# First layer's attention: scores by quarters of the array, one score bank per head

## The chip, the cores and the metric

The kernel is one program on one core of a Trainium2 chip. Its time is the device time of an execution in microseconds; of several runs the median counts. A profile of one execution gives each instruction its start and length.

## What is computed

The reference is a network of two layers on `x` of 4 x 1024 tokens with 128 features. Each layer has an attention and a mixture of experts, each behind a LayerNorm whose output is scaled and shifted per batch entry and each gated before it is added back. The change touches the first layer's attention alone: 16 heads of 64 features, a window of 64 tokens back, and a bias that grows with the distance.

```python
q = rmsnorm(x @ wq.T, q_norm_w)          # over all 16 * 64 features
k = rmsnorm(x @ wk.T, k_norm_w)
v = x @ wv.T
scores = einsum('bhqd,bhkd->bhqk', q, k) * HD ** -0.5
scores = scores + slopes[:, None, None] * dist      # dist = key - query
scores = where((dist > 0) | (dist < -64), -inf, scores)
out = einsum('bhqk,bhkd->bhqd', softmax(scores), v) @ wo.T
```

## The kernel before, in words

The whole program keeps `x` in SBUF and runs stage after stage; between two stages all engines meet. The stage here is `window_attention_stage`. It treats two heads at a time, a *pair*: 64 features of head 0 on partitions 0 to 63, 64 of head 1 on partitions 64 to 127. There are 4 batch entries x 8 pairs = 32 pairs. A pair's 1024 queries fall into 16 blocks of 64, and a block sees the 128 keys that end with its own 64 (`kk`, `k_pad`, has 64 columns of zeros ahead of the first key). Four blocks are one *step*; a pair has four steps (r = 0 to 3 in the code, steps 1 to 4 in the text), the stage 128.

Each engine's program is written out as a loop over g, the number of the step, and works at several steps at once:

- TensorE (PE), in iteration g: the scores of g (L734); the projections for the next pair (`project`, L714 and L717: two of q in step 1, two of k in step 2, half of v in steps 3 and 4 each); the transposes of the probabilities of g - 2 (L745, `probsT_ps`); the output products of g - 3 (L760, `o_ps`, each head in its half of the array's columns, on its 64 partitions of the result); after step 4 of a pair the wo products of the pair before (L773).
- ScalarE (ACT): the evacuation of the projections from PSUM (q L819, k L824, v L826), then the four exponentials of g (L869, with their sums), then the copy `oT` of the output products of g - 3 (L877).
- VectorE (DVE): the second head's half of the q evacuation (L892), then bias, mask and row minimum of the scores of g (they are held negated) in one custom instruction per block with a read-out of the minimum behind it (L960, `s_biased` and `s_min`), the reciprocal of the sums of g - 1 (L966), the copy of the transposed probabilities of g - 2 (L972).
- GpSimd (POOL): the normalisation of the probabilities (L989). SyncE: a DMA that shifts v by 64 tokens (`v_shift`).

The order of work is thus fixed by the loops; semaphores (`s_mm`, `biased`, `exped`, `rsum`, `normed`, `turned`, `pt_out`, `pv_mm`, `o_out`, `a_out`) hold an engine until another has counted far enough. Into the pairs of batch entries 1 to 3 the loops also sow the next stage's work on the batch entry before (`routed`, `route`: LayerNorm statistics, POOL's rstd at L145, the normalised tiles `hk` at L155, transposes at L680, the router's logits and tables), at fixed steps.

The scores of a block are one 128 x 128 product. Its weights are a block-diagonal table `qbd` (`q_bd`): columns 0 to 63 hold head 0's queries in partitions 0 to 63, columns 64 to 127 head 1's queries in partitions 64 to 127, the other two quarters are zero. So a product yields 64 queries of head 0 on partitions 0 to 63 and 64 of head 1 on 64 to 127, against 128 keys. ACT writes one quarter and DVE the other; POOL has zeroed the table ahead of the stage. The four products of a step fill one PSUM bank of two (`sp_[g % 2]`):

```python
if g >= 2:
    pe.wait_ge(biased, g - 1)
for i in range(4):
    j = 4 * r + i
    m = nc.tensor.matmul(sp_[g % 2][:, i, :], qbd[:, h % 2, j, :],
                         kk[:, h % 2, BLK * j:BLK * j + P], start=True, stop=True)
```

In the trace a float32 product has two records of PE (and two weight loads, PEld).

Of the kernel before, what the change touches and what calls it, by code (L numbers as in the profile page):

```python
# [35 lines left out]
NBLK = T // BLK  # L36
RMS_EPS = 1e-6
# [530 lines left out]
def window_attention_stage(nc, K, A, gram, hq, hk, M, N1, N2, aff_in):  # L568
# [3 lines left out]
    with ExitStack() as st:  # L572
# [4 lines left out]
        nbias = K.sb("nbias", [P, PAIRS, P], ctx=st)  # L577
# [3 lines left out]
        qbd = K.sb("q_bd", [P, 2, NBLK, P], ctx=st)  # L581
# [14 lines left out]
        def fill(pool):  # L596

            for n, dst in enumerate((qbd[:].rearrange("p a b c -> p (a b c)"), kk[:, :, 0:BLK], vs[0:BLK, :, 0, :])):
# [12 lines left out]
        def scale_q(dve):  # L611
# [21 lines left out]
        (h_in, p_mm, a_out, q_out, v_sh0, v_sh1, s_mm, biased, exped, rsum, normed, turned, pt_out, pv_mm, o_out,  # L633
         wo_mm, wo_gated, x_added, prob_set, scaled, shifted) = K.sems(
            st, "win", "h_in", "proj_mm", "act_out", "q_out", "v_shift_even", "v_shift_odd", "score_mm", "biased",
            "exp", "rsum", "normed", "turned", "probsT_out", "pv_mm", "o_out", "wo_mm", "wo_gated", "x_added", "probs_set",
            "scaled", "shifted")
# [31 lines left out]
        with nc.Block() as block:  # L669
            @block.tensor  # L670
            def _(pe):
# [24 lines left out]
                def project(n):  # L696
# [3 lines left out]
                    if n >= 2:  # L700

                        hh, uu = units[n - 2]
                        pe.wait_ge(a_out, n - 1)
                        if uu in (0, 1):
                            pe.wait_ge(q_out, 2 * hh + uu + 1)
# [18 lines left out]
                for g in range(G + 4):  # L724
                    h, r = divmod(g, GRP)
                    if g < G:
                        if r == 0:
                            pe.wait_ge(a_out, out_count(h, 3))
                            pe.wait_ge(q_out, 2 * h + 2)
                        if g >= 2:  # L730
                            pe.wait_ge(biased, g - 1)
                        for i in range(4):
                            j = 4 * r + i
                            m = nc.tensor.matmul(sp_[g % 2][:, i, :], qbd[:, h % 2, j, :],  # L734
                                                 kk[:, h % 2, BLK * j:BLK * j + P], start=True, stop=True)
                        m.then_inc(s_mm, 1)
# [10 lines left out]
                    if 3 <= g < G + 3:  # L747
# [31 lines left out]
            def _(act):  # L779
# [26 lines left out]
                def evacuate(n):  # L806
# [49 lines left out]
                for g in range(G + 3):  # L856
# [4 lines left out]
                    if g < G:  # L861
                        act.wait_ge(biased, g + 1)
                        if g == 0:
                            act.wait_ge(prob_set, 1)
                        if g >= 3:
                            act.wait_ge(turned, g - 2)
                        for i in range(4):
                            own = slice(BLK if g % GRP == 0 and i == 0 else 0, P)
                            r = nc.scalar.activation(pr[:, g % 3, i, own], sb_[:, g % 2, i, own], ACT.Exp, scale=-1.0,  # L869
# [12 lines left out]
            def _(dve):  # L882
                v = nc.vector

                def evacuate(n):
                    h, u = units[n]
                    if u not in (0, 1):
                        return
                    dve.wait_ge(p_mm, n + 1)
                    if u == 0 and h >= 2:  # L890
                        dve.wait_ge(s_mm, GRP * (h - 1))
# [4 lines left out]
                for n in range(6):  # L896
                    evacuate(n)
                v.memset(pr[:, :, 0, 0:BLK], 0.0).then_inc(prob_set, 1)
# [49 lines left out]
                for g in range(G + 2):  # L948
# [3 lines left out]
                    for n in unit_steps(g):  # L952
                        evacuate(n)
                    if g < G:
                        dve.wait_ge(s_mm, g + 1)
                        if g >= 2:
                            dve.wait_ge(exped, g - 1)
                        for i in range(4):
                            own = slice(BLK if 4 * r + i == 0 else 0, P)
                            q = v.tensor_tensor_reduce(sb_[:, g % 2, i, own], sp_[g % 2][:, i, own],  # L960
                                                       nbias[:, h % PAIRS, own], 1.0, 3e38, ALU.add, ALU.min,
                                                       mn[:, g % 4, i:i + 1])
# [15 lines left out]
            def _(pool):  # L978
                M.constants(pool)
                for g in range(G):  # L980
# [9 lines left out]
                    if g % 2 == 1 and g // 2 < FILLS:  # L990
                        if g == 1:
                            pool.wait_ge(filled, 4)
# [1505 lines left out]
def constants():  # L2498
# [5 lines left out]
    neg = np.empty((2, BLK, PAIRS, P), np.float32)  # L2504
    ok = (dist <= 0) & (dist >= -WIN)
    for h in range(H0):
        neg[h % 2, :, h // 2, :] = np.where(ok, -slopes[h] * dist, 1e30)
# [8 lines left out]
    return {"identity": np.eye(P, dtype=np.float32), "neg_bias": neg.reshape(P, PAIRS, P),  # L2516
# [46 lines left out]
```

## Time and profile before

| | us |
|---|---|
| runs shown: median of 3 (lowest, highest) | 2058.07 (2057.89, 2059.19) |
| span of the profiled execution, first to last instruction | 2056.4 |
| PE / PEld busy | 1579.5 / 917.7 |
| DVE / ACT / POOL busy | 1339.0 / 1135.7 / 550.2 |
| first and last score product of the stage start at | 87.1 and 606.6 |

The profiled execution's own device time is not listed apart from the three runs; its span lies 1.5 to 2.8 us below them. A share of busy time is a mean over the whole span. What an engine is worth in one stage is read in that stage, from the work in order of time: a row there has the start and length of an instruction (or of several alike, "x8"), its engine and line, what it writes and reads, and in brackets how long its engine sat idle before it and which instruction ended that.

### The profile page before, as it was taken

The page shows a single profiled execution, that of the slowest core. Times are in us where ns is not written, and L with a number is a line of the kernel's source. Part 1 is how long each engine was busy: PE and PEld are TensorE (multiplying, and loading weights), DVE is VectorE, ACT ScalarE, POOL GpSimd, SP SyncE. Part 2 cuts the span into 40 slices and gives each one's busy share as a digit, 9 for nine tenths or more (in the row PEclk, how much of TensorE's full clock was granted, in tenths as well). Part 3 has the DMA queues.
Part 4 walks back from the last instruction along what each step waited for, and adds up shares of the span by engine and source line. Part 5 has one row for each costly group of instructions (what it writes and reads, how often), then busy time and mean ns, then how long its engine had stood idle before and what let it go on. Part 6 is the DMA issues. An engine that isn't in the chain of part 4 may idle for free. (4 is left out here: it accounts for less than half of the span.)

```text
span 2056.4 us, 34421 instructions
## 1 busy us (share of the span) xinstructions
PE 1579.5 (77%) x11512; PEld 917.7 (45%) x11512; DVE 1339.0 (65%) x3318; ACT 1135.7 (55%) x2965; POOL 550.2 (27%) x615
## 2 busy tenths in 40 slices
PE   6799999999991699245999999999999735424910
PEld 3478777777771699221222222222222234323910
DVE  5655656656564322267999999999999287842523
ACT  3366766666651344142688888888888733111300
POOL 2133323524526400571001001001000020372056
PEclk9799999999995799666899999999999967556965
DMA  5144311211101676142000000000000000013832
GB/s 191 39 156 156 107 30 36 54 28 43 42 21 37 203 234 205 52 122 83 23 21 26 18 26 18 27 18 26 19 25 2 1 0 6 21 45 124 253 91 72
DMA packets 86203, 138.99 MB, mean 68 GB/s; under 512 B 18084, under 2 KB 57252, under 8 KB 85900
## 3 DMA queue, kind: packets, MB, share of 16 engines
q1 hardware_dynamic: 62860, 92.08, 15.2%
q0 software_dynamic: 11936, 34.49, 5.1%
q10 hardware_dynamic: 11232, 10.23, 1.4%
q8 instruction: 93, 1.52, 0.3%
q14 instruction: 82, 0.67, 0.1%
HBM read 75.51 MB, written 45.11 MB: 59 GB/s over the span
## 5 line engine op out<-in xcount | busy, mean ns | idle before, releaser
L2062 DVE TENSOR_REDUCE q_max<-s_ps 128x1 f32<-128x1024 f32 x512 | 598.2, 1219 | 14.0 <-PE s_ps L1953 6.8
L2043 ACT ACTIVATE probs<-s_ps 128x512 f32<-128x512 f32 x1024 | 535.5, 603 | 124.5 <-PE s_ps L1974 124.3
L1953 PE MATMUL s_ps<-k_stack,q_stack 64*128 64x512 bf16 x1024 | 351.2, 397 | 16.9 <-PEq L96 8.5
L1974 PE MATMUL s_ps<-q_stack,k_stack 64*128 64x512 bf16 x1024 | 319.5, 384 | 20.2 <-ACT probs L2043 15.8
L1988 PE MATMUL o_ps<-probs,v_aug 128*32 128x512 f32 x2048 | 273.6, 606 | 0.7 <-ACT probs L2043 0.7
L1974 PEld LDWEIGHTS s_ps<-q_stack,k_stack 64*128 64x128 bf16 x1024 | 78.6, 94 | 333.9 <-ACT probs L2043 281.9
L989 POOL TENSOR_TENSOR probs<-probs,p_rsum 128x512 f32<-128x512 f32 x128 | 132.9, 1038 | 325.8 <-DVE p_rsum L966 325.1
L869 ACT ACTIVATE probs<-s_biased,s_min 128x128 f32<-128x128 f32 (+1 forms) x512 | 197.7, 391 | 37.0 <-DVE s_min L960 35.6
L734 PE MATMUL score_ps<-k_pad,q_bd 128*128 128x128 f32 x1024 | 146.7, 287 | 0.0
L960 DVE CUSTOM_DVE_ANT_0 s_biased<-score_ps,nbias 128x128 f32<-128x128 f32 (+1 forms) x512 | 115.8, 282 | 41.8 <-PE score_ps L734 40.6
L1580 POOL CAST neg_max_parts<-neg_max 16x128 bf16<-16x128 f32 x32 | 9.0, 281 | 474.7 <-DVE neg_max L2070 474.7
L734 PEld LDWEIGHTS score_ps<-k_pad,q_bd 128*128 128x128 f32 x1024 | 125.9, 194 | 7.4 <-issue 1.0
L1953 PEld LDWEIGHTS s_ps<-k_stack,q_stack 64*128 64x128 bf16 x1024 | 77.5, 94 | 113.2 <-DVE q_max L2062 104.3
L892 DVE TENSOR_SCALAR q_bd<-proj_ps,qscale 64x512 f32<-64x512 f32 x64 | 48.4, 756 | 107.9 <-PE proj_ps L714 104.7
L1474 ACT ACTIVATE moe0b_hid<-moe0b_hps,moe0b_wblock 128x256 f32<-128x256 f32 x156 | 66.9, 473 | 82.5 <-PE moe0b_hps L1429 80.7
L972 DVE COPY probsT<-probsT_ps 128x512 f32<-128x512 f32 x128 | 86.7, 677 | 37.0 <-PE probsT_ps L745 36.4
L1619 POOL DMA_INDIRECT moe0g_yg<-moe_rows,moe_slot x64 | 66.4, 1038 | 157.9 <-POOLq L96 139.0
L869 ACT ACTIVATION_READ_ACCUMULATOR probs<-s_biased,s_min 128x1 f32 x512 | 98.0, 191 | 0.0
L1538 POOL DMA_INDIRECT moe1g_yg<-moe_rows,moe_slot x64 | 61.2, 956 | 121.3 <-PEq L1533 102.1
L819 ACT ACTIVATE q_bd<-proj_ps,qscale 64x512 f32<-64x512 f32 x64 | 43.7, 683 | 84.9 <-PE proj_ps L714 84.8
L1498 DVE TENSOR_TENSOR moe0b_y<-moe0b_yps,moe0b_wblock 128x256 f32<-128x256 f32 x39 | 16.6, 425 | 99.6 <-PE moe0b_yps L1439 99.6
L760 PE MATMUL o_ps<-probsT,v_shift 128*64 128x64 f32 x1024 | 73.5, 235 | 8.8 <-ACT oT L877 8.6
(315 smaller groups left out, 2824.5 us busy)
## 6 DMA issues: line engine op xcount, KB each, us to landing
moe0b_wblock<-in_L_ffn_blocks SPq DMA_DIRECT2D x39, 578.0 KB, 3.9
moe_rows<-zero_rows POOLq DMA_DIRECT2D x18, 960.0 KB, 4.4
moe1b_wblock<-in_L_ffn_blocks SPq DMA_DIRECT2D x39, 256.0 KB, 3.5
v_shift<-v_tiles SPq DMA_DIRECT2D x32, 256.0 KB, 3.1
v_shift<-v_tiles SPq DMA_DIRECT2D x32, 224.0 KB, 3.6
qk_parts_dram<-qk_parts SPq DMA_DIRECT2D x16, 384.0 KB, 2.7
q_stack<-qk_parts_dram SPq DMA_DIRECT2D x192, 32.0 KB
k_stack<-qk_parts_dram SPq DMA_DIRECT2D x192, 32.0 KB
```

Source lines behind the costliest of these rows:

```text
L734: m = nc.tensor.matmul(sp_[g % 2][:, i, :], qbd[:, h % 2, j, :], kk[:, h % 2, BLK * j:BLK * j + P], start=True, stop=True)
L760: m = nc.tensor.matmul(op[a * BLK:(a + 1) * BLK, i, :], src[:, a * HD0:(a + 1) * HD0], pt[:, k % 2, i, a * BLK:(a + 1) * BLK], start=True, ...
L869: r = nc.scalar.activation(pr[:, g % 3, i, own], sb_[:, g % 2, i, own], ACT.Exp, scale=-1.0, bias=mn[:, g % 4, i:i + 1], accum_out=sm[:, g ...
L960: q = v.tensor_tensor_reduce(sb_[:, g % 2, i, own], sp_[g % 2][:, i, own], nbias[:, h % PAIRS, own], 1.0, 3e38, ALU.add, ALU.min, mn[:, g ...
L972: v.tensor_copy(pt[:, k % 2], tp[:]).then_inc(pt_out, 1)
L989: nc.gpsimd.tensor_tensor(pb, pb, bc(ri[:, g % 4, :], 2, P), ALU.mult).then_inc(normed, 1)
L1474: nc.scalar.activation(hid[:, j % 2, f, :], hp[n % 4][:, 0:BR], gelu, bias=bias).then_inc(g_out, 1)
L1953: mm = nc.tensor.matmul(s1[u % 2][:, c * CH:(c + 1) * CH], qs[head_rows(m), quad % 4, j, qt * P:(qt + 1) * P], ks[head_rows(m), quad % 4, ...
L1974: nc.tensor.matmul(bank_of("exp", 4 * k + pos)[:], ks[head_rows(m), quad % 4, j, kt * P:(kt + 1) * P], qs[head_rows(m), quad % 4, j, half ...
L1988: m = nc.tensor.matmul(op[32 * h:32 * h + 32, :], va[:, quad % 2, kt, h, :], pr[:, k % 2, h, :], start=(kt == 0), stop=(kt == TPB - 1))
L2043: nc.scalar.activation(pr[:, k % 2, HEADS[pos], :], bank_of("exp", n)[:], ACT.Exp).then_inc(sm["exp"], 1)
L2062: v.tensor_reduce(mx[:, h % 4, col:col + 1], s1[u % 2][:], AX.X, ALU.max).then_inc(sm["maxed"], 1)
```

## The change

Query blocks are no longer laid out block-diagonally. ACT writes all 128 partitions of plain q (`qh`, `q_heads`), and DVE's half of the q evacuation goes, with its semaphore. A block's scores are two products, one per head, of 64 features by 64 queries against 128 keys. A step has eight. Head a works in rows 64a to 64a + 63 of the array, block i in columns 64 (i % 2) and up, so that four products in a row lie in the four quarters. Head a writes to bank `sp_[a]`: blocks i = 0 and 1 on the lower and upper 64 partitions of columns 0 to 127, blocks 2 and 3 likewise in columns 128 to 255. Both banks belong to the step in hand, so the scores of g now wait for the bias of g - 1.

As a slot of 128 x 128 scores now holds two blocks of one head, the bias table has a row of 128 keys for each of 16 heads on both halves of the partitions (twice the bytes). DVE still takes four slots a step; in step 1 the block without earlier keys lies beside one that has them, so a slot there is split in two halves, its masked part of `s_biased` being set by a small memset (`MASKED`), and ACT's exponentials run over the whole slot. The output products pick their probabilities by head and half.

```diff
-        nbias = K.sb("nbias", [P, PAIRS, P], ctx=st)
+        nbias = K.sb("nbias", [P, H0, P], ctx=st)
...
-        qbd = K.sb("q_bd", [P, 2, NBLK, P], ctx=st)
+        qh = K.sb("q_heads", [P, 2, T], ctx=st)
...
@@ tensor
                         if r == 0:
                             pe.wait_ge(a_out, out_count(h, 3))
-                            pe.wait_ge(q_out, 2 * h + 2)
-                        if g >= 2:
-                            pe.wait_ge(biased, g - 1)
+                        if g >= 1:
+                            pe.wait_ge(biased, g)
                         for i in range(4):
                             j = 4 * r + i
-                            m = nc.tensor.matmul(sp_[g % 2][:, i, :], qbd[:, h % 2, j, :],
-                                                 kk[:, h % 2, BLK * j:BLK * j + P], start=True, stop=True)
+                            for a in range(2):
+                                hd = slice(a * HD0, (a + 1) * HD0)
+                                m = nc.tensor.matmul(sp_[a][i % 2 * BLK:(i % 2 + 1) * BLK, i // 2, :],
+                                                     qh[hd, h % 2, BLK * j:BLK * (j + 1)],
+                                                     kk[hd, h % 2, BLK * j:BLK * j + P], start=True, stop=True)
...
                                 m = nc.tensor.matmul(op[a * BLK:(a + 1) * BLK, i, :], src[:, a * HD0:(a + 1) * HD0],
-                                                     pt[:, k % 2, i, a * BLK:(a + 1) * BLK], start=True, stop=True)
+                                                     pt[:, k % 2, 2 * a + i // 2, i % 2 * BLK:(i % 2 + 1) * BLK],
+                                                     start=True, stop=True)
@@ scalar
-                        r = nc.scalar.activation(
-                            qbd[0:BLK, h % 2, half * 8:half * 8 + 8, 0:BLK],
-                            pj[n % 2][0:BLK, :].rearrange("p (j q) -> p j q", q=BLK), ACT.Copy,
-                            scale=qs[0:BLK, h % PAIRS:h % PAIRS + 1])
+                        r = nc.scalar.activation(qh[:, h % 2, half * CH:(half + 1) * CH], pj[n % 2][:], ACT.Copy,
+                                                 scale=qs[:, h % PAIRS:h % PAIRS + 1])
@@ vector
-                def evacuate(n):
...
-                    v.tensor_scalar(qbd[BLK:P, h % 2, u * 8:u * 8 + 8, BLK:P],
-                                    pj[n % 2][BLK:P, :].rearrange("p (j q) -> p j q", q=BLK),
-                                    qs[BLK:P, h % PAIRS:h % PAIRS + 1], None, ALU.mult).then_inc(q_out, 1)
...
+                def biased_scores(g, a, s, rows, cols):
+
+                    i, hd = 2 * a + s, g // GRP % PAIRS * 2 + a
+                    return v.tensor_tensor_reduce(sb_[rows, g % 2, i, cols], sp_[a][rows, s, cols],
+                                                  nbias[rows, hd, cols], 1.0, 3e38, ALU.add, ALU.min,
+                                                  mn[rows, g % 4, i:i + 1])
...
-                    for n in unit_steps(g):
-                        evacuate(n)
                     if g < G:
-                        dve.wait_ge(s_mm, g + 1)
                         if g >= 2:
                             dve.wait_ge(exped, g - 1)
...
+                        if r == 0:
+
+                            for a in range(2):
+                                v.memset(sb_[0:BLK, g % 2, 2 * a, 0:BLK], MASKED)
+                        dve.wait_ge(s_mm, g + 1)
+                        for a in range(2):
+                            for s in range(2):
+                                if r == 0 and s == 0:
+                                    biased_scores(g, a, s, slice(0, BLK), slice(BLK, P))
+                                    q = biased_scores(g, a, s, slice(BLK, P), slice(0, P))
+                                else:
+                                    q = biased_scores(g, a, s, slice(0, P), slice(0, P))
                         q.then_inc(biased, 1)
```

On PE the order of the blocks stays, only the score block differs. Step 2 of a pair up to the next score block, before (`score_ps` scores, `proj_ps` projections, `probsT_ps` transposes, `o_ps` output products):

```order
L734 MATMUL score_ps<-k_pad,q_bd 128x128 x4
L714 MATMUL proj_ps<-hk,wkT 128x512 x2
L745 MATMUL probsT_ps<-ident,probs 128x128 x4
L760 MATMUL o_ps<-probsT,v_shift 64x64 x2
L760 MATMUL o_ps<-probsT,v_tiles 64x64 x2
L760 MATMUL o_ps<-probsT,v_shift 64x64 x2
L760 MATMUL o_ps<-probsT,v_tiles 64x64 x2
L734 MATMUL score_ps<-k_pad,q_bd 128x128 x4
```

and with the change:

```order
L731 MATMUL score_ps<-k_pad,q_heads 64x128 x8
L710 MATMUL proj_ps<-hk,wkT 128x512 x2
L743 MATMUL probsT_ps<-ident,probs 128x128 x4
L758 MATMUL o_ps<-probsT,v_shift 64x64 x2
L758 MATMUL o_ps<-probsT,v_tiles 64x64 x2
L758 MATMUL o_ps<-probsT,v_shift 64x64 x2
L758 MATMUL o_ps<-probsT,v_tiles 64x64 x2
L731 MATMUL score_ps<-k_pad,q_heads 64x128 x8
```

Four products over the whole array became eight over a quarter each, between the same neighbours.

On DVE, step 1 of a pair before (`q_bd` the q evacuation, `s_biased` the bias, `s_min` the read-out of the minimum):

```order
L972 COPY probsT<-probsT_ps 128x512
L892 TENSOR_SCALAR q_bd<-proj_ps,qscale 64x8x64 x2
L960 ISA s_biased,s_min<-score_ps,nbias 128x64
L960 ISA s_min 128x1
L960 ISA s_biased,s_min<-score_ps,nbias 128x128
L960 ISA s_min 128x1
```

and with the change:

```order
L962 COPY probsT<-probsT_ps 128x512
L944 MEMSET s_biased 64x64 x2
L882 ISA s_biased,s_min<-score_ps,nbias 64x64
L882 ISA s_min 64x1
L882 ISA s_biased,s_min<-score_ps,nbias 64x128
L882 ISA s_min 64x1
L882 ISA s_biased,s_min<-score_ps,nbias 128x128
```

The two evacuations, which wait for the q projections of the same step on PE, no longer stand ahead of the bias; two memsets do, and two slots take two instructions each.

## Rows read from the trace of the kernel before

**Rows 1.** The page, busy time, share of the span and instructions of each engine.

```profile
PE 1579.5 (77%) x11512; PEld 917.7 (45%) x11512; DVE 1339.0 (65%) x3318; ACT 1135.7 (55%) x2965; POOL 550.2 (27%) x615
```

**Rows 2.** Line L734: durations in ns, first and last start in us.

```profile
L734 PE MATMUL score_ps<-k_pad,q_bd x1024: 273/276/582, 87.1 to 606.6; 128*128 128x128 f32 x171
```

**Rows 3.** Busy us (and instructions) of PE, PEld, DVE, ACT, POOL; PEclk; DMA share, GB/s.

```profile
162.06:177.91 15.85, 15.65 (x155) 12.66 (x153) 8.27 (x42) 10.65 (x42) 5.66 (x6) 1.00 0.45 156
```

**Rows 4.** One pair in order of time, PE: start us, length us, line, [idle before].

```profile
162.06 1.06 PE L734 MATMUL score_ps<-k_pad,q_bd 128*128 128x128 f32 x8
162.96 1.88 PE L714 MATMUL proj_ps<-hq,wqT 128*128 128x512 f32 x4
164.68 0.60 PE L745 MATMUL probsT_ps<-ident,probs 128*128 128x128 f32 x4
165.21 0.34 PE L760 MATMUL o_ps<-probsT,v_shift 128*64 128x64 f32 x4
...
165.49 0.29 PE L760 MATMUL o_ps<-probsT,v_shift 128*64 128x64 f32 x4
165.60 0.29 PE L760 MATMUL o_ps<-probsT,v_tiles 128*64 128x64 f32 x4
165.82 1.16 PE L734 MATMUL score_ps<-k_pad,q_bd 128*128 128x128 f32 x8
166.82 1.88 PE L714 MATMUL proj_ps<-hk,wkT 128*128 128x512 f32 x4
...
169.68 1.16 PE L734 MATMUL score_ps<-k_pad,q_bd 128*128 128x128 f32 x8
170.68 1.06 PE L717 MATMUL proj_ps<-wvT,nat 128*128 128x128 f32 x8
...
175.41 0.34 PE L760 MATMUL o_ps<-probsT,v_shift 128*64 128x64 f32 x4 [0.20 <-ACT oT L877]
...
177.91 1.06 PE L734 MATMUL score_ps<-k_pad,q_bd 128*128 128x128 f32 x8
```

**Rows 5.** The same pair, ACT, steps 3 and 4.

```profile
172.88 0.58 ACT L826 COPY v_tiles<-proj_ps 128x512 f32<-128x512 f32 x1 [1.69 <-issue]
...
174.91 0.35 ACT L877 COPY oT<-o_ps 128x256 f32<-128x256 f32 x1
```

**Rows 6.** Waits of PE, 92 to 605 us: in total, times, longest.

```profile
PE o_ps L760 <- ACT oT L877: 7.9, 26, 0.7
```

**Rows 7.** The same pair in order of time, DVE and ACT in step 1.

```profile
164.02 1.61 DVE L892 TENSOR_SCALAR q_bd<-proj_ps,qscale 64x512 f32<-64x512 f32 x2 [3.93 <-PE proj_ps L714]
...
165.67 0.23 DVE L960 CUSTOM_DVE_ANT_0 s_biased<-score_ps,nbias 128x64 f32<-128x64 f32 x1
...
166.57 0.35 ACT L869 ACTIVATE probs<-s_biased,s_min 128x64 f32<-128x64 f32 x1 [1.00 <-DVE s_min L960]
```

**Rows 8.** Second layer's attention in order of time, PE.

```profile
1301.57 0.39 PE L1974 MATMUL s_ps<-q_stack,k_stack 64*128 64x512 bf16 x1
1301.57 0.39 PE L1953 MATMUL s_ps<-k_stack,q_stack 64*128 64x512 bf16 x1
1301.89 1.06 PE L1988 MATMUL o_ps<-probs,v_aug 128*32 128x512 f32 x8
1302.89 0.39 PE L1974 MATMUL s_ps<-q_stack,k_stack 64*128 64x512 bf16 x1
```

**Rows 9.** A pair with LayerNorm of the batch before, in order of time.

```profile
280.55 0.17 DVE L161 SCALAR_TENSOR_TENSOR n0bb_shift<-n0bb_mv,n0bb_rstd 128x8 f32<-128x8 f32 x1 [2.17 <-POOL n0bb_rstd L145]
...
284.43 0.88 ACT L155 ACTIVATE hk<-nat,n0bb_shift,n0bb_rstd 128x128 f32<-128x128 f32 x2
...
285.41 0.30 PE L680 MATMUL proj_ps<-ident,hk 128*128 128x128 f32 x1 [2.10 <-issue]
```

**Rows 10.** Busy time by engine, PEclk and DMA around that wait.

```profile
284.00:288.00 4.00, 2.59 (x26) 2.19 (x27) 0.97 (x4) 1.54 (x6) 1.04 (x1) 0.77 0.02 4
```

**Rows 11.** Busy time by engine, PEclk and DMA ahead of the stage.

```profile
44.00:48.00 4.00, 4.00 (x16) 1.13 (x14) 2.11 (x4) 0.00 (x0) 0.00 (x0) 1.00 0.03 8
```

More of the change, by code:

```diff
@@ L36 @@
 NBLK = T // BLK
+MASKED = 1e30
 RMS_EPS = 1e-6
@@ L596, in fill @@
         def fill(pool):
-            for n, dst in enumerate((qbd[:].rearrange("p a b c -> p (a b c)"), kk[:, :, 0:BLK], vs[0:BLK, :, 0, :])):
+            for n, dst in enumerate((kk[:, :, 0:BLK], vs[0:BLK, :, 0, :])):
                 nc.gpsimd.memset(dst, 0.0).then_inc(filled, 1)
@@ L632, in window_attention_stage @@
         wp = [K.ps(f"wo_ps{i}", [P, CPT, D], st) for i in range(2)]
[L633 to L637, printed above, removed]
+        (h_in, p_mm, a_out, v_sh0, v_sh1, s_mm, biased, exped, rsum, normed, turned, pt_out, pv_mm, o_out,
+         wo_mm, wo_gated, x_added, scaled, shifted) = K.sems(
+            st, "win", "h_in", "proj_mm", "act_out", "v_shift_even", "v_shift_odd", "score_mm", "biased",
+            "exp", "rsum", "normed", "turned", "probsT_out", "pv_mm", "o_out", "wo_mm", "wo_gated", "x_added", "scaled", "shifted")
         v_sh = (v_sh0, v_sh1)
@@ L867, in _ @@
                         for i in range(4):
-                            own = slice(BLK if g % GRP == 0 and i == 0 else 0, P)
-                            r = nc.scalar.activation(pr[:, g % 3, i, own], sb_[:, g % 2, i, own], ACT.Exp, scale=-1.0,
+                            r = nc.scalar.activation(pr[:, g % 3, i, :], sb_[:, g % 2, i, :], ACT.Exp, scale=-1.0,
                                                      bias=mn[:, g % 4, i:i + 1], accum_out=sm[:, g % 4, i:i + 1])
@@ L883, in _ @@
                 v = nc.vector
-                def evacuate(n):
[L886 to L891, printed above, removed]
-                    v.tensor_scalar(qbd[BLK:P, h % 2, u * 8:u * 8 + 8, BLK:P],
-                                    pj[n % 2][BLK:P, :].rearrange("p (j q) -> p j q", q=BLK),
-                                    qs[BLK:P, h % PAIRS:h % PAIRS + 1], None, ALU.mult).then_inc(q_out, 1)
-                for n in range(6):
-                    evacuate(n)
-                v.memset(pr[:, :, 0, 0:BLK], 0.0).then_inc(prob_set, 1)
+                def biased_scores(g, a, s, rows, cols):
[3 more added lines that the diff above has]
+                                                  mn[rows, g % 4, i:i + 1])
                 def routed(g):
@@ L951, in _ @@
                     h, r = divmod(g, GRP)
-                    for n in unit_steps(g):
-                        evacuate(n)
                     if g < G:
-                        dve.wait_ge(s_mm, g + 1)
                         if g >= 2:
                             dve.wait_ge(exped, g - 1)
[L958 to L962, printed above, removed]
+                        if r == 0:
[9 more added lines that the diff above has]
+                                    q = biased_scores(g, a, s, slice(0, P), slice(0, P))
                         q.then_inc(biased, 1)
@@ L991, in _ @@
                         if g == 1:
-                            pool.wait_ge(filled, 4)
+                            pool.wait_ge(filled, 3)
                         clear_rows(pool, g // 2)
@@ L2503, in constants @@
     dist = c - BLK - r
-    neg = np.empty((2, BLK, PAIRS, P), np.float32)
+    neg = np.empty((2, BLK, H0, P), np.float32)
     ok = (dist <= 0) & (dist >= -WIN)
     for h in range(H0):
-        neg[h % 2, :, h // 2, :] = np.where(ok, -slopes[h] * dist, 1e30)
+        neg[:, :, h, :] = np.where(ok, -slopes[h] * dist, MASKED)
     lower = (np.arange(E)[None, :] < np.arange(E)[:, None]).astype(np.float32).reshape(1, -1)
@@ L2514, in constants @@
     steps = np.concatenate([np.arange(E) * SPAN, np.arange(STEPS_OF) * BR, np.arange(NBK)]).astype(np.float32)
-    return {"identity": np.eye(P, dtype=np.float32), "neg_bias": neg.reshape(P, PAIRS, P),
+    return {"identity": np.eye(P, dtype=np.float32), "neg_bias": neg.reshape(P, H0, P),
             "lower": np.ascontiguousarray(lower), "before": before, "steps": steps}
```

5 lines of the change are left out of this document (removed).

## The prediction

> **What bounds the kernel now.** I started with the page. TensorE (PE) is the busiest engine, 1579.5 us or 77% of the span [rows 1], but that is a mean over many stages, so I went to the stage that the change touches. Its score products run from 87.1 to 606.6 us [rows 2], 128 steps of four query blocks, four steps to a pair of heads, 32 pairs. In one undisturbed pair, from one first score product to the next, PE is busy 15.65 of 15.85 us, at the full granted clock, while VectorE (DVE) has 8.27 us of work, ScalarE (ACT) 10.65 and GpSimd (POOL) 5.66 [rows 3]. So here PE's own work sets the time. Then I read that pair in order of time [rows 4], looking for the start of each block of products and the one wait: the second engine in line shows there. In the fourth step the output products wait 0.20 us for ACT's copy `oT`; over the stage that happens 26 times, 7.9 us [rows 6].
>
> **The score block.** Of old, four products take eight records. After the wo products, whose tiling is the same, the block lasts 162.96 - 162.06 = 0.90 us, so 0.112 a record; after the output products, which use half the array's columns each, 166.82 - 165.82 = 1.00 [rows 4]. That 0.10 more is the first record paying for a change of tiling.
>
> New, eight products of 64 x 64 give sixteen records that stream as many columns as before (128). If the four quarters run side by side, four records pass in the time of one: 16 / 4 x 0.112 = 0.45 us plus edges. The nearest row is the output block: also eight products and sixteen records, of half the columns, two side by side, hence the same ideal length. Four of its records take 165.60 - 165.49 = 0.11 us, the last four 0.22 until the next block starts, the whole block 165.82 - 165.21 = 0.61 [rows 4]. I take 0.61 for the new block.
>
> That quarters overlap is not in the trace as such; its two halves are. Four column strips of a float32 product start together: eight records of 512 columns between 1301.89 and 1302.89, 0.125 each, where one alone streams 4 x 0.112 = 0.45. Products on the upper and lower 64 rows start in the same hundredth of a microsecond (1301.57, twice) [rows 8]. The bounds of the block are 0.61 (four side by side), 16 / 2 x 0.112 + 0.16 = 1.06 (two), and 16 x 0.112 + 0.16 = 1.95 (none); I take the first because both halves are nearest to it.
>
> A rule speaks against. The Trainium skill ("TensorE: Matmul & The Clock Gate", Part 3) says that a weight load overlaps running products only where their row groups differ. By it two quarters on the same rows would take turns, and the block would be the 1.06 of the two-sided case (2069 in all, below). The output products share all 128 rows and still run in pairs [rows 4], so here the trace disagrees; I keep that case as a rival.
>
> **Sum over a pair.**
> - Step 1 (after wo, before the 512-column q projections): 0.90 becomes 0.61, plus 0.10 for the new change of tiling after wo: -0.19.
> - Step 2 (before the k projections): 1.00 becomes 0.61. The penalty of the first record moves to a 512-column product, whose second weights have time to load: -0.39.
> - Step 3 (before the v projection, 128 columns): -0.39, and 0.10 returns as that projection's first record: -0.29.
> - Step 4: -0.29 in the same way, but it buys nothing. ACT's evacuation of v (172.88) waits for the output products of step 3; the four exponentials and `oT` (174.91) follow, and the output products of step 4 wait for that (175.41) [rows 4, 5]. From step 3's output products to step 4's this chain is as long as before. PE's wait becomes about 0.20 + 0.29 = 0.5 us.
>
> Sum: -0.87 us a pair. The first and last pair are paced by waits (no previous pair, no projections); I give them -0.3 each. 30 x 0.87 + 0.6 = 26.7, say -27 us.
>
> Does ACT also bind step 3? By the same rows, moved: when the k projections end, ACT has a copy and four exponentials (174.91 - 172.88 = 2.03), `oT` (0.35) and some 0.3 for the hand-overs ahead of it, 2.7 us; PE meanwhile transposes (0.53), multiplies (0.61), scores (0.61), projects v (1.0) and transposes again (0.53), 3.3 [rows 4, 5]. Half a microsecond of slack stays.
>
> **The rest of the edit.** DVE loses its half of the q evacuation, 1.61 us a pair, which today stands ahead of the biased scores of step 1: these start at 165.67, 2.7 us after their products were done, and ACT's first exponential waits 1.00 for them [rows 7]. It gains two small memsets and two more half-height bias passes, below 0.5 us, in idle time. So rsum, POOL's normalisation and ACT's exponentials of step 1 come 1 to 2 us sooner. On the plain pairs this only buys slack. It counts three times, where the next stage's LayerNorm rides along: POOL's rstd is queued behind that normalisation, DVE's shift waits 2.17 for it, ACT's last `hk` tile ends at 285.31 and the transposes wait 2.10 [rows 9]. That chain moves up by about 2.2 us, 0.87 of which is in the sum: 3 x 1.3 = -4. In that gap the granted clock falls (0.77 of full over 284 to 288) [rows 10]; a shorter gap may save up to 1 us each. I leave this in the range.
>
> **The added wait.** One bank per head means one score set, not two: the scores of step g now wait for the bias of g - 1, formerly g - 2. Behind a held score stand the projection, the transposes and all later PE work. In a plain pair DVE is done about 1.1 us after the score block, and PE needs at least 0.10 + 0.9 + 0.53 + 0.61 = 2.1 to come back, so it costs nothing. That cover is too short only after a routing step on DVE of over some 1.5 us ahead of a step without wo; a handful of such steps per batch, a few tenths each: +1 us.
>
> At nothing: the bias table is twice as large, but DMA is idle from 44 us (8 GB/s) and the table is wanted after 87 [rows 2, 11]; POOL's fill of the old q table falls away in the same stretch; the exponentials of step 1 cover the masked half too (0.05 us of ACT, where it has slack).
>
> In all -27 - 4 + 1 = -30 us on the profiled span of 2056.4. The median of the runs, 2058.07, lies 1.7 above that span; I subtract from the median: **2028 us**.
>
> **Rivals.**
> - *Only two quarters overlap* (slower). Block 1.06: step 1 +0.26, step 2 +0.06, step 3 +0.16, step 4 +0.16 inside its wait: some +0.48 x 31 = +15, less 4: **2069**. It decides once the block exceeds about 0.9 us. With no overlap, 1.95, the same sum gives +4.0 a pair, about 2180. Against it: [rows 4, 8]. Chance 0.11.
> - *The waits take more* (ACT or the single bank paces step 3 too). Then steps 2 and 3 give nothing and step 1's 0.19 x 31 = 6 and the 4 of the LayerNorm remain: **2048**. For it: the wait on `oT` already stands in 26 pairs [rows 6]; against it, the half microsecond of slack. Chance 0.15.
> - *Step 4 pays too*, if ACT's v evacuation finds a way forward: 0.29 x 31 = 9 more: **2019**. Against it: it waits for step 3's products by program order [rows 5]. Chance 0.07.
> - *The change is not what it says*: if the eight products were laid on the whole array, sixteen records in turn, that is the 1.95 above. Included there.
>
> **How the numbers follow.** Forecast 0.67, waits 0.15, step 4 0.07, too little overlap 0.11. The forecast alone spans 2019 (block at 0.5, clock kept) to 2039 (block at 0.75). The range takes in the third rival, 2017, and most of the second, to 2046; about 0.17 stays outside. A measurement of this kernel tells about 0.2%, 4 us. The forecast, the second and third case lie below 2054 save for a small part of the second (0.03): faster 0.86, same 0.04, slower 0.10.
>
> **What would show it.** Right: score records in fours a hundredth apart, a block of 0.6; step 1's biased scores straight after their products; PE's wait on `oT` up from 7.9 to some 16 us, in nearly every pair; score products ending near 576 instead of 606.6. Wrong: records in pairs 0.11 apart and a block over 0.9; waits of the score products for `s_biased`; a clock below full in the stage; other stages moved by more than 1 us.

## The result and the profile after

The changed kernel takes 2030.55 us, the median of four runs (2027.98 to 2032.33), against 2057.98 (2057.7 to 2059.19, four runs) for the kernel before on the same chip: a ratio of 0.9871, 95% interval 0.9857 to 0.9885. That is 27.4 us, or 1.3%, faster. The forecast was 2028, with a range of 2017 to 2046.

The profiled execution is the one of 2027.98 us, the fastest of the four, 2.6 below their median; its span is 30.2 us shorter than before. The page:

```profile
span 2026.2 us, 36468 instructions
...
PE 1542.1 (76%) x12536; PEld 853.5 (42%) x12536; DVE 1317.3 (65%) x3445; ACT 1138.4 (56%) x2965; POOL 546.1 (27%) x614
```

PE's busy time is 37 us less than before [rows 1] although it has 1024 more matmul records, DVE's is 22 less. The score line, with durations in ns and first and last start in us:

```profile
L731 PE MATMUL score_ps<-k_pad,q_heads x2048: 269/269/321, 85.6 to 576.6; 64*64 64x128 f32 x187
```

From first to last start it is 491.0 us, 519.5 before [rows 2], so about 28 of the 30 us lie inside the stage. Some 1.5 came ahead of it and the rest behind; neither is put down to the change. Ahead of the stage TensorE has the same work; only GpSimd's fill of the old table falls away, and the bias table has twice the bytes. Over the runs below, the first score product starts between 85.5 and 86.9 us in the five that carry the change and between 85.8 and 86.8 in the four that do not, so the 1.5 us lie within what profiles differ by. They are part of why the score products end at 576.6, near the 576 that the prediction named.

The plain pair that starts at 157.57, in columns as in [rows 3]:

```profile
157.57:172.72 15.15, 14.65 (x185) 10.85 (x184) 7.61 (x46) 10.81 (x42) 5.64 (x6) 1.00 0.48 165
```

A pair takes 15.15 us in place of 15.85. The same pair in order of time on PE, as in [rows 4]:

```profile
157.57 0.67 PE L731 MATMUL score_ps<-k_pad,q_heads 64*64 64x128 f32 x16
158.17 1.98 PE L710 MATMUL proj_ps<-hq,wqT 128*128 128x512 f32 x4
159.99 0.60 PE L743 MATMUL probsT_ps<-ident,probs 128*128 128x128 f32 x4
160.52 0.34 PE L758 MATMUL o_ps<-probsT,v_shift 128*64 128x64 f32 x4
...
161.14 0.67 PE L731 MATMUL score_ps<-k_pad,q_heads 64*64 64x128 f32 x16
161.74 1.98 PE L710 MATMUL proj_ps<-hk,wkT 128*128 128x512 f32 x4
163.56 0.60 PE L743 MATMUL probsT_ps<-ident,probs 128*128 128x128 f32 x4
...
164.70 0.67 PE L731 MATMUL score_ps<-k_pad,q_heads 64*64 64x128 f32 x16
165.30 1.16 PE L713 MATMUL proj_ps<-wvT,nat 128*128 128x128 f32 x8
...
167.44 0.67 PE L731 MATMUL score_ps<-k_pad,q_heads 64*64 64x128 f32 x16
...
170.13 0.34 PE L758 MATMUL o_ps<-probsT,v_shift 128*64 128x64 f32 x4 [0.50 <-ACT oT L871]
...
170.74 2.05 PE L772 MATMUL wo_ps<-woT_gated,oT 128*128 128x128 f32 x16
```

From a score block to the next work it is 0.60 us each time, where it was 0.90 or 1.00. The trace's single records, which this view draws together, start in fours 7 ns apart, and the last three fours follow each other by 0.109 us: four quarters at a time. But both 512-column projections have grown from 1.88 to 1.98, and PE now waits 0.50 us for `oT` in step 4, where it waited 0.20.

From the start of one score block to the next:

| | step 1 | step 2 | step 3 | step 4 | pair |
|---|---|---|---|---|---|
| before | 3.76 | 3.86 | 3.03 | 5.19 | 15.84 |
| after | 3.56 | 3.56 | 2.74 | 5.29 | 15.15 |
| difference | -0.20 | -0.30 | -0.29 | +0.10 | -0.69 |
| forecast | -0.19 | -0.39 | -0.29 | 0 | -0.87 |

PE's waits from 92 to 576 us (in total, times, longest):

```profile
PE o_ps L758 <- ACT oT L871: 14.5, 29, 0.8
PE proj_ps L680 <- issue: 3.0, 3, 1.0
PE score_ps L731 <- DVE s_min L882: 3.0, 5, 1.1
```

The wait on `oT` went from 7.9 us in 26 places [rows 6] to 14.5 in 29. The wait of the single bank is small, 3.0 us. ACT ahead of `oT`, as in [rows 5]:

```profile
167.60 0.59 ACT L823 COPY v_tiles<-proj_ps 128x512 f32<-128x512 f32 x1 [1.46 <-issue]
...
169.63 0.35 ACT L871 COPY oT<-o_ps 128x256 f32<-128x256 f32 x1
```

From the copy of v to the end of `oT` it is 2.38 us, as before: this chain has not become shorter. DVE in step 1:

```profile
158.31 0.22 DVE L882 CUSTOM_DVE_ANT_0 s_biased<-score_ps,nbias 64x64 f32<-64x64 f32 x1 [2.79 <-PE score_ps L731]
...
158.55 0.29 DVE L882 CUSTOM_DVE_ANT_0 s_biased<-score_ps,nbias 64x128 f32<-64x128 f32 x1
...
159.63 0.29 DVE L882 CUSTOM_DVE_ANT_0 s_biased<-score_ps,nbias 128x128 f32<-128x128 f32 x1
...
159.85 0.17 DVE L956 RECIPROCAL p_rsum<-p_sum 128x4 f32<-128x4 f32 x1
```

The bias starts 0.14 us after the score block is done, where it waited 2.7 us behind the q evacuation [rows 7]; the six passes take 159.85 - 158.31 = 1.54 us. One of the three pairs that carry LayerNorm, in order of time:

```profile
269.02 0.88 ACT L156 ACTIVATE hk<-nat,n0bb_shift,n0bb_rstd 128x128 f32<-128x128 f32 x2 [0.29 <-DVE n0bb_shift L162]
...
272.70 0.88 ACT L156 ACTIVATE hk<-nat,n0bb_shift,n0bb_rstd 128x128 f32<-128x128 f32 x2
...
273.67 0.63 PE L680 MATMUL proj_ps<-ident,hk 128*128 128x128 f32 x4 [1.01 <-issue]
```

The transposes wait 1.01 us in place of 2.10 [rows 9], and the granted clock around that wait stays at 1.00, the higher of its two levels (2.4 GHz), where a mean of 0.77 between the two stood after the longer wait [rows 10]:

```profile
270.00:274.00 4.00, 2.91 (x45) 2.30 (x44) 2.54 (x20) 3.54 (x13) 2.08 (x2) 1.00 0.00 0
274.00:278.00 4.00, 3.87 (x55) 3.27 (x53) 1.63 (x9) 2.55 (x9) 0.00 (x0) 1.00 0.02 4
```

The 28 us of the stage add up: 30 plain shares of 0.69 (-20.7); beyond that share, the three LayerNorm pairs (20.65, 19.67 and 20.70 us before; 17.60, 17.66 and 17.66 now) -6.0, and five pairs with routing steps (16.08 to 16.21 before; 15.15, one 15.23, now) -1.4; the first pair -0.1; the last one +0.4.

### The profile page after: what moved, and what is told of

The parts are those of the page before. It is cut to its first block and busy times, and to the rows that moved or that the text cites. A ratio compares the mean times of both kernels' runs of the same rounds, so it can differ in the third digit from the quotient of the medians.

```text
span 2026.2 us, 36468 instructions
## 1 busy us (share of the span) xinstructions
PE 1542.1 (76%) x12536; PEld 853.5 (42%) x12536; DVE 1317.3 (65%) x3445; ACT 1138.4 (56%) x2965; POOL 546.1 (27%) x614
## 5 line engine op out<-in xcount | busy, mean ns | idle before, releaser
L882 DVE CUSTOM_DVE_ANT_0 s_biased<-score_ps,nbias 128x128 f32<-128x128 f32 (+2 forms) x576 | 137.6, 280 | 112.1 <-PE score_ps L731 109.5
L863 ACT ACTIVATE probs<-s_biased,s_min 128x128 f32<-128x128 f32 x512 | 199.0, 394 | 6.2 <-DVE s_min L882 5.0
L818 ACT ACTIVATE q_heads<-proj_ps,qscale 128x512 f32<-128x512 f32 x64 | 44.0, 688 | 80.0 <-PE proj_ps L710 79.9
L731 PE MATMUL score_ps<-k_pad,q_heads 64*64 64x128 f32 x2048 | 85.4, 282 | 3.3 <-DVE s_min L882 3.0
L743 PE MATMUL probsT_ps<-ident,probs 128*128 128x128 f32 x512 | 77.4, 274 | 1.1 <-POOL probs L979 0.9
L1429 PEld LDWEIGHTS moe0b_yps<-moe0b_wblock,moe0b_hid 128*128 128x128 f32 x624 | 75.6, 192 | 2.0
```

The source lines that it names most:

```text
L731: m = nc.tensor.matmul(sp_[a][i % 2 * BLK:(i % 2 + 1) * BLK, i // 2, :], qh[hd, h % 2, BLK * j:BLK * (j + 1)], kk[hd, h % 2, BLK * j:BLK * ...
L743: m = nc.tensor.transpose(tp[:, i, :], pr[:, k % 3, i, :], K.ident[:])
L863: r = nc.scalar.activation(pr[:, g % 3, i, :], sb_[:, g % 2, i, :], ACT.Exp, scale=-1.0, bias=mn[:, g % 4, i:i + 1], accum_out=sm[:, g % 4 ...
L882: return v.tensor_tensor_reduce(sb_[rows, g % 2, i, cols], sp_[a][rows, s, cols], nbias[rows, hd, cols], 1.0, 3e38, ALU.add, ALU.min, mn[r ...
```

## The experiments

Theory: the four quarters run at once (some 0.7 us a pair), DVE's vanished evacuation speeds up the LayerNorm pairs and pays for the single bank, and ACT's order of work hides what step 4 saves. Rivals: the gain hangs on the products' order, or comes mostly from DVE, or step 4 is held by something else.

**Does the order of the quarters matter?** All four blocks of head 0, then all of head 1. In the program's order only two quarters then have work at a time.

```diff
-                        for i in range(4):
-                            j = 4 * r + i
-                            for a in range(2):
+                        for a in range(2):
+                            for i in range(4):
+                                j = 4 * r + i
```

> The changed kernel with the eight score products in another order: head 0's four blocks first, then head 1's, so that neighbours in the program share their 64 rows and only the two column quarters alternate. If the gain rests on four quarters side by side and TensorE takes products in program order, only two run at a time: the score block goes from 0.60 to about 1.05 us, steps 1 to 3 lose 0.45 each, step 4 hides it in its wait on oT: 1.35 x 31 = +42, about 2072 us. If TensorE looks past the products ahead, or the block's length comes from the weight loads alone (sixteen of them, as many as in the output block), the block stays at 0.60 and the time at 2030.

Measured: 2032.54 us (2031.52 to 2034.31), ratio 0.9882 (0.9865 to 0.9898), level with the change. Step 2's scores on PE:

```profile
161.17 0.68 PE L731 MATMUL score_ps<-k_pad,q_heads 64*64 64x128 f32 x16
161.78 1.55 PE L710 MATMUL proj_ps<-hk,wkT 128*128 128x512 f32 x3
```

The block takes 0.61 us, and its single records again start in fours, now within 33 ns. If products started strictly in their order, head 1's first two could start only with head 0's last two: six rounds of 0.109 at the least instead of four, 0.65 us, and some 0.82 with the 0.16 that the block takes besides its rounds (0.60 - 4 x 0.109). The trace does not say which record belongs to which product, but 0.61 is too short for that: by the times, products of head 1 start while some of head 0, ahead of them in the program, still wait. So the theory that the order matters fell. The working takes a record of 128 columns to hold its quarter for 0.109 us, as it holds the whole array for 0.112. No run changes the columns and keeps the sixteen weight loads, so it stays open whether the columns or the loads set the pace of the rounds, the other way out that the expectation named.

**The single bank's wait alone**, in the kernel before:

```diff
-                        if g >= 2:
-                            pe.wait_ge(biased, g - 1)
+                        if g >= 1:
+                            pe.wait_ge(biased, g)
```

> The kernel before with one edit: the scores of step g wait for the bias of g - 1 instead of g - 2, as if there were one set of score banks. My theory: in step 1 the bias stands behind VectorE's two q evacuations and ends at 166.5 in the pair that I read, 0.7 us after the scores of step 2 start today; with the hand-over +0.8 x 31 = +25, about 2083 us, and TensorE's waits for s_min appear in nearly every pair. The rival, that the added wait costs nothing by itself: 2058, no such waits.

Measured: 2077.64 us (2076.69 to 2079.24) against 2057.28, ratio 1.0099 (1.0082 to 1.0116). PE's waits from 92 to 620 us:

```profile
PE score_ps L734 <- DVE s_min L960: 24.1, 35, 1.0
```

Step 1 grows from 3.76 to 4.52 us in every plain pair: the scores of step 2 wait for a bias that stands behind the evacuation. With one bank, the evacuation is on PE's path. The time lies 5 us under the expectation: the LayerNorm pairs, 20.65, 19.67 and 20.70 us before, take 19.63 to 19.67, and the routing pairs take in part of the wait.

**DVE's order alone**, in the kernel before: the q evacuation behind the bias and the reciprocal; work and banks as they were.

```diff
-                    for n in unit_steps(g):
-                        evacuate(n)
                     if g < G:
...
                         v.reciprocal(ri[:, (g - 1) % 4, :], sm[:, (g - 1) % 4, :]).then_inc(rsum, 1)
+                    for n in unit_steps(g):
+                        evacuate(n)
```

> The kernel before with VectorE's half of the q evacuation moved behind the bias and the reciprocal of the same step; products, banks and waits as before. It is the part of the change on VectorE alone. My theory: plain pairs stay at 15.85 us, the pairs that carry the LayerNorm and the router of the batch before get shorter, as they did in the change beyond the 0.69 of a plain pair: 4 to 8 us in all, 2050 to 2054. If those pairs got shorter through the shorter score blocks instead: 2058.

Measured: 2046.77 us (2045.58 to 2048.32), ratio 0.9948 (0.9932 to 0.9965). The plain pairs stay at 15.84, the LayerNorm pairs fall to 17.41 each (from 20.65, 19.67, 20.70), and four of the five routing pairs to 15.84. PE's waits from 92 to 605 us:

```profile
PE proj_ps L680 <- issue: 0.8, 3, 0.3
```

Ten microseconds thus come from DVE's order alone, with no quarter of the array in it, and all of them in a handful of pairs.

**DVE's half of q put back** into the changed kernel, ahead of the bias as it was (ACT writes the lower half only, with a semaphore for PE):

```diff
+                    v.tensor_scalar(qh[BLK:P, h % 2, u * CH:(u + 1) * CH], pj[n % 2][BLK:P, :],
+                                    qs[BLK:P, h % PAIRS:h % PAIRS + 1], None, ALU.mult).then_inc(q_out, 1)
...
                     h, r = divmod(g, GRP)
+                    for n in unit_steps(g):
+                        evacuate(n)
                     if g < G:
```

> The changed kernel with the second head's half of the q evacuation given back to VectorE, ahead of the bias, as before the change; quarters and single banks stay. My theory: the bias of step 1 then ends about 1 us after TensorE could start the scores of step 2, and with a single set of banks they wait for it: +1.1 x 31 = +34, and 5 more in the pairs with LayerNorm: about 2068, no better than before. If the removal on VectorE is only tidying: 2030 to 2036.

Measured: 2094.05 us (2093.38 to 2096.75), ratio 1.0182 (1.0165 to 1.0199): 64 us more than the change, and slower than the kernel before. The expectation had it at 2068. PE's waits from 92 to 640 us:

```profile
PE score_ps L735 <- DVE s_min L899: 61.3, 41, 2.7
```

DVE and PE at the end of one step 1, in order of time:

```profile
185.40 1.61 DVE L890 TENSOR_SCALAR q_heads<-proj_ps,qscale 64x512 f32<-64x512 f32 x2 [3.96 <-PE proj_ps L713]
...
187.09 0.19 DVE L963 MEMSET s_biased<- 64x64 f32 x2
...
188.82 0.17 DVE L975 RECIPROCAL p_rsum<-p_sum 128x4 f32<-128x4 f32 x1
...
188.96 0.67 PE L735 MATMUL score_ps<-k_pad,q_heads 64*64 64x128 f32 x16 [1.68 <-DVE s_min L899]
```

Step 1 grows from 3.56 to 5.32 us. Memsets, six passes and their read-outs take 188.82 - 187.09 = 1.73 us, which now all lie behind the evacuation and ahead of the scores. The expectation had the scores wait 1.1 us; they wait 1.68 and step 1 grows by 1.76, 0.66 us more in each of 31 pairs, 20 of the 26 us that the expectation lacks. Three plain pairs also grew by another 1.70 in step 2. There the k projections take 3.52 us in place of 1.82, at a granted clock near its lower level (1.2 GHz); in step 1 ahead of them, with its idle 1.69 us, it had still been 1.00. The stretch from the k projections to the transposes in one of the three, in columns as in [rows 3]:

```profile
223.37:226.89 3.52, 3.52 (x9) 1.36 (x5) 1.04 (x10) 1.88 (x8) 2.34 (x3) 0.52 0.48 186
```

Three times 1.70 is 5 us more. So the quarters and the single bank pay only where DVE's evacuation does not stand ahead of the bias. Whether it had to go, or would do no harm behind the bias, as in the bias-first run, was not tried in the changed kernel.

**ACT's exponentials ahead of its v evacuation**, in the iteration that serves steps 3 and 4, in the changed kernel:

```diff
-                    for n in unit_steps(g):
-                        evacuate(n)
+                    late = g % GRP == 2 and g < G
+                    if not late:
+                        for n in unit_steps(g):
+                            evacuate(n)
...
                         r.then_inc(exped, 1)
+                    if late:
+                        for n in unit_steps(g):
+                            evacuate(n)
```

> The changed kernel; on ScalarE, in step 3 of each pair, the four exponentials go ahead of the evacuation of v, which waits for that step's output products. My theory: step 4 gave nothing because its output products wait for oT behind that evacuation and the exponentials (0.57 us of wait a pair now). With the exponentials already done the wait goes: step 4 pays 0.5 x 31 = 15, about 2015 us. Rival: something else (POOL's normalisation, the single banks) takes its place, and less than 5 us come.

Measured: 2019.35 us (2018.26 to 2019.72) against 2058.74, ratio 0.9807 (0.9791 to 0.9824), the fastest of all. One pair, in columns as in [rows 3], and PE's waits from 92 to 576 us:

```profile
156.61:171.19 14.58, 14.58 (x185) 10.82 (x184) 7.63 (x46) 10.93 (x42) 5.65 (x6) 1.00 0.48 170
```

```profile
PE score_ps L731 <- DVE s_min L887: 3.2, 5, 1.1
...
PE o_ps L758 <- ACT oT L876: 2.9, 10, 0.6
```

ACT around the hand-over from step 3 to step 4:

```profile
167.10 0.57 ACT L823 COPY v_tiles<-proj_ps 128x512 f32<-128x512 f32 x1
167.57 0.37 ACT L876 COPY oT<-o_ps 128x256 f32<-128x256 f32 x1
168.27 0.59 ACT L823 COPY v_tiles<-proj_ps 128x512 f32<-128x512 f32 x1 [0.33 <-PE proj_ps L713]
```

`oT` starts 167.57 - 156.61 = 10.96 us after the pair's first scores, where it was 169.63 - 157.57 = 12.06. Step 4 falls from 5.29 to 4.72, and PE has no idle time left in the pair. Some pairs with routing steps keep a part (15.40 to 15.63), and the time lies 4 us above the 2015 that was expected.

**The same edit in the kernel before:**

> The same edit of ScalarE's order alone, in the kernel before. My theory: the same chain is already there, 0.27 us of wait in most pairs: 0.27 x 29 = 8, about 2049 us. Rival (it binds only behind the shorter blocks): 2057.

Measured: 2053.25 us (2049.8 to 2054.49, six runs), ratio 0.9969 (0.9956 to 0.9981). Plain pairs fall by 0.27, to 15.57. But the LayerNorm pairs gain nothing (20.70, 20.71, 20.50; the middle one, 19.67 before, now has a granted clock of 0.50 from 416.56 to 419.97), two routing pairs lose half a microsecond (16.21 to 16.69 and 16.68), and the transposes still wait two microseconds in each LayerNorm pair (waits of PE, 92 to 601 us):

```profile
PE proj_ps L680 <- issue: 6.3, 3, 2.1
```

**The scores of step 4 twice, and the scores of step 2 twice**, in the changed kernel (sixteen more records in one step of each pair; the edit for step 4, with `r == 1` for step 2):

```diff
-                        for i in range(4):
+                        for i in range(8 if r == 3 else 4):
+                            i = i % 4
```

> The changed kernel with the eight score products of step 4 made twice (the same values into the same place), 0.44 us more on TensorE in every pair. My theory: step 4 has 0.57 us of wait on oT, which takes it in: under 4 us more, 2030 to 2034. If TensorE's own work set the end of step 4 too: +0.44 x 32 = +14, 2044.

> The same doubling in step 2 instead. My theory: TensorE's own work sets step 2, so all of it shows: +0.44 x 31 = +14, about 2044 us. If the chain through ScalarE set the whole pair: 2030.

Measured: step 4 doubled, 2036.49 us (2032.55 to 2036.59), ratio 0.989 (0.9874 to 0.9907); step 2 doubled, 2045.01 (2041.96 to 2046.57), ratio 0.993 (0.9913 to 0.9946). Step 4 doubled, PE in one pair, and its waits from 92 to 576 us:

```profile
168.07 1.10 PE L732 MATMUL score_ps<-k_pad,q_heads 64*64 64x128 f32 x32
169.10 1.16 PE L713 MATMUL proj_ps<-wvT,nat 128*128 128x128 f32 x8
...
173.35 0.67 PE L732 MATMUL score_ps<-k_pad,q_heads 64*64 64x128 f32 x16
```

```profile
PE o_ps L759 <- ACT oT L872: 3.5, 9, 0.6
```

Step 2 doubled, PE in one pair:

```profile
163.63 1.10 PE L732 MATMUL score_ps<-k_pad,q_heads 64*64 64x128 f32 x32
164.66 1.98 PE L710 MATMUL proj_ps<-hk,wkT 128*128 128x512 f32 x4
...
167.63 0.67 PE L732 MATMUL score_ps<-k_pad,q_heads 64*64 64x128 f32 x16
```

The same 0.43 us of work costs nothing in step 4 (173.35 - 168.07 = 5.28, as without it; the wait on `oT` shrinks by 11 us), and all of itself in step 2 of a plain pair (4.00 in place of 3.56). With step 2 doubled the stage of the profiled run grew by 11.9 us, since the three LayerNorm pairs take the work in (17.62 to 17.67); the medians differ by 14.5. With step 4 doubled the stage of the profiled run grew by 2.3 us, 1.1 of it in three pairs with routing and 1.1 in the last pair, where the granted clock is 0.50 from 575.30 to 578.70 (in the change's own last pair it is 1.00 throughout). The median grew by 5.9, 2.5 us above the range that was expected. The other 3.6 stay open; the runs of the change itself lie 4.4 apart.

**The old products with both orders mended**, bias first on DVE and exponentials first on ACT:

> The kernel before (block-diagonal products, two sets of banks) with both edits of order: VectorE's q evacuation behind bias and reciprocal, ScalarE's exponentials of step 3 ahead of the evacuation of v. It is the version with exponentials first (2019 us) without the quarters. My theory: the two orders add up, plain pairs 15.57 us as in the edit on ScalarE alone, the pairs with LayerNorm near 17.1: 10 + 8 less, about 2040 us; the quarters are then worth 15.57 - 14.58 = 0.99 a pair where no wait hides any of it, some 21 to 30 us in all. Rival: most of the gain of the changed kernel was order, and this lands below 2030.

Measured: 2038.33 us (2038.02 to 2039.59) against 2059.21, ratio 0.9901 (0.9884 to 0.9917). Plain pairs take 15.57 us, LayerNorm pairs 16.90. With the same two hand-overs mended, the quarters (with their single bank) against block diagonal are 14.58 against 15.57 in a plain pair, 0.99 us, and 2019.35 against 2038.33 in all: 19 us, less than the 21 to 30 expected. In the profiled runs the stage differs by 21.6: the quarters do not shorten the LayerNorm pairs, which take 17.02 to 17.07 with them, and shorten some routing pairs by less (15.85 to 15.40).

## Why the prediction was right, point by point

The time, the sign and the mechanism held. That the sum held so closely is partly luck: the plain shares came out 6 us too small, and gains that stood outside the sum, in the pairs with LayerNorm and routing, made up 3 of them.

**The score block: right.** 0.61 was predicted, 0.60 measured. The rival in which only two quarters overlap would have shown records in pairs and a block of 1.06; there is no such block. On the rule that spoke against, the Trainium skill also says ("TensorE: Matmul & The Clock Gate", Part 2) that products stay in program order and only weight loads are pulled ahead. The head-by-head run disagrees, as far as times can tell: its block of 0.61 us is too short for that order.

**Step 2: this is the term that failed.** The text said that the first record's penalty "moves to a 512-column product, whose second weights have time to load" and booked nothing for it. The k projections went from 168.54 - 166.82 = 1.72 us to 163.56 - 161.74 = 1.82, so step 2 gave 0.30, not 0.39. It is the first weights that are not hidden. Before, PEld starts to load them 0.11 us ahead of the product, while the last scores pass; with the change it starts together with the product, and the second record starts 0.53 us behind the first instead of 0.43. Before (two rows) and after (one):

```profile
166.71 0.30 PEld L714 LDWEIGHTS proj_ps<-hk,wkT 128*128 128x128 f32 x2
168.54 0.60 PE L745 MATMUL probsT_ps<-ident,probs 128*128 128x128 f32 x4
```

```profile
161.73 0.30 PEld L710 LDWEIGHTS proj_ps<-hk,wkT 128*128 128x128 f32 x2 [0.17 <-issue]
```

The q projections of step 1 did the same (159.99 - 158.17 = 1.82), which the sum did not have either. Steps 1 and 2 thus keep two penalties of 0.10 that I had taken for hidden, 0.18 of the 0.87 a pair: some 5.5 us over the stage. The other two, after wo and before v, were in the sum and came: wo's block is 172.72 - 170.74 = 1.98, 1.89 before, and the table has that 0.10 in step 4 where the working had it in step 1. The Trainium skill ("TensorEngine Tiling (Array Packing)", Key Properties) says that a change of tiling mode drains TensorE; the trace agrees, with 0.10 us in front of a 128- and a 512-column product alike.

**Step 3: right**, -0.29 as predicted, and ACT did not bind it.

**Step 4: right.** The saving turned into PE's wait: 0.50 us in the pair, as forecast, 14.5 us over the stage where "some 16" stood. The runs show the cover from three sides: twice the products in step 4 cost a plain pair nothing, twice those in step 2 cost their full time, and with ACT's exponentials ahead of v step 4 falls by 0.57. The rival "step 4 pays too" needed a reason for v to find a way forward; the way turned out to be the reverse, v standing back.

**The evacuation that falls away: right in kind and, as far as it went, in size.** Predicted -4 in the LayerNorm pairs; measured -6.0 there and -1.4 in five routing pairs that I had not looked at. In the kernel before, two of the three LayerNorm pairs have a stretch at the lower clock behind their wait of 2.1 us (a granted clock of 0.50 from 286.2 to 289.6 and from 555.8 to 559.2), and the middle one, with the same wait, has none. The first and the middle pair, in columns as in [rows 3]:

```profile
273.25:293.90 20.65, 18.42 (x163) 14.92 (x161) 9.20 (x47) 13.73 (x48) 5.75 (x5) 0.92 0.12 29
408.45:428.12 19.67, 16.97 (x162) 13.63 (x161) 9.16 (x47) 13.42 (x48) 6.83 (x6) 1.00 0.13 33
```

The pair at full clock went from 19.67 to 17.66 us, 2.0, of which 0.7 is the plain share: the 1.3 of the prediction, and 4 in three pairs. The other two were 1.0 us longer before, and with the change the granted clock is 1.00 over all three pairs: that is the other 2, which the prediction had left in the range. How many of the pairs fall to the lower clock differs between profiles: all three do in the run with ACT's order mended in the kernel before, behind the same wait. The bias-first run shows the same pairs falling with the old products. Alone that is 10 us, the clock included; beside the quarters some 7, since a LayerNorm pair of the change, 17.6 us, is still longer than the 17.41 of that run: its transposes wait about a microsecond each, against 0.3.

**The added wait: right in size, for a partly wrong reason.** Predicted +1; the score products wait 3.0 us in five places, up to 1.1. In three routing pairs step 3 grew by 0.4 to 0.7 us and step 4 shrank by nearly as much, since its wait on `oT` was there to give; only the last pair lost some 0.4. The slack in a plain pair is real but was mispriced: in step 1 the bias ends 159.85 - 158.17 = 1.7 us after the score block, not 1.1. It still ends well ahead of PE's return to the scores at 161.14; with the evacuation back in front of it, it does not.

**In all:** about -21 for the plain shares (the first pair's -0.1 with them) in place of -26.7, -7.4 in place of -4 (4 as predicted, 2 of the clock, 1.4 in the routing pairs), +0.4 in place of +1, which is the -28 of the stage. A median 2.6 us above the profiled run is within what the runs differ by.

Not tried: two score sets inside the two banks, which might take the remaining 3 us of waits on `s_min`.

## What to carry to other kernels

Where products fill only part of the array, put them side by side in its quarters, and charge a fixed price for every change of tiling to the product that follows, however long it is; here it was 0.10 us, as the weights no longer loaded ahead of the product. Before counting a saving on the busiest engine, look for the wait that ends last behind it: the same 0.3 us was worth all of itself in one step and nothing in another until a second engine's order was changed. When an edit takes work off an engine with slack, look at what stood behind that work in its queue; here that alone was 10 us, and with that work left in front the rest of the change loses 37.

## What the runs showed of the hardware that was not expected

- A change of tiling costs the following 128 x 128 product 0.10 us whether it streams 128 columns (1.06 to 1.16) or 512 (1.88 to 1.98): the product's first weight load, which had started 0.11 us ahead of it, now starts with it.
- By the times, TensorE looks past a waiting product: eight products in head order took 0.61 us, as in the interleaved order (0.60), where strict order would take some 0.82 by the working above.
- On DVE, half the partitions save nothing, half the columns little: this custom pass took 0.29 us on 128 x 128, 0.29 on 64 x 128 and 0.22 on 64 x 64, each with a read-out of about 0.08 behind it; with two of a step's four slots split, its bias took 1.54 us (158.31 to 159.85).
